# P*V of two key tiles back to back at each second key tile, in an attention and mixture-of-experts kernel on one core

## The reference, cut to what matters

```
kv = (ckv @ wkv_b)                       # ckv: 64 latent numbers per token
scores = einsum('bhqd,bhkd->bhqk', qs, ks_) * scale
scores = where(causal, scores, min)
attn = softmax(scores, axis=-1)
out = einsum('bhqk,bhkd->bhqd', attn, v)
return out @ wo
```

## Time and profile before

| what | value |
|---|---|
| time, median of 3 runs | 1330.67 us (1329.75 to 1333.64) |
| span of the profiled execution, first to last instruction | 1335.4 us |
| own time of the profiled execution | not recorded beside its span |
| PE busy | 1184.3 us, 89% |
| DVE, ACT, POOL busy | 61%, 60%, 55% |
| mean granted TensorE clock | 0.968 |

### The profile page before, as it was taken

One profiled execution on the slowest core, in us unless ns is written; L12 is line 12 of the kernel. 1 busy time (PEld: TensorE's weight loads), 2 busy tenths in 40 slices (PEclk: granted clock), 3 DMA queues, 4 the chain that ended last, 5 costly groups with the idle time before them and its releaser, 6 DMA issues. The chain is left out here.

```text
span 1335.4 us, 20034 instructions
## 1 busy us (share of the span) xinstructions
PE 1184.3 (89%) x6808; PEld 554.4 (42%) x6819; DVE 819.6 (61%) x1846; ACT 796.1 (60%) x1237; POOL 733.9 (55%) x444
## 2 busy tenths in 40 slices
PE   4988999999998999999999899999999999588820
PEld 3533555444443543434433533333333335266610
DVE  6565677657658765565657775566655516455546
ACT  3634663766664567666666467777777782265532
POOL 0055540564553266666676077878778891435545
PEclk9998999999999999999999999999999999799965
DMA  9035200110111010000011001000000000256744
GB/s 291 22 93 134 75 1 1 54 27 16 26 39 32 8 47 18 11 20 12 16 32 41 13 12 44 25 24 15 10 24 25 24 1 16 63 152 190 184 133 134
DMA packets 63031, 70.27 MB, mean 53 GB/s; under 512 B 10080, under 2 KB 52448, under 8 KB 62816
## 3 DMA queue, kind: packets, MB, share of 16 engines
q1 hardware_dynamic: 56656, 56.26, 14.8%
q0 software_dynamic: 4864, 10.51, 3.4%
q10 hardware_dynamic: 1424, 2.38, 0.7%
HBM read 37.51 MB, written 14.83 MB: 39 GB/s over the span
## 5 line engine op out<-in xcount | busy, mean ns | idle before, releaser
L561 POOL TENSOR_TENSOR D<-D,B 128x1024 f32<-128x1024 f32 (+3 forms) x256 | 513.0, 2004 | 140.8 <-ACT B L753 124.1
L1114 DVE TENSOR_REDUCE mxp<-ps 128x1 f32<-128x512 f32 (+3 forms) x640 | 385.4, 609 | 272.3 <-PE ps L1661 196.5
L753 ACT ACTIVATE B<-ps 128x1024 f32<-128x1024 f32 (+1 forms) x320 | 286.0, 894 | 224.2 <-PE ps L1690 150.6
L1711 PE MATMUL ps<-B,kv 128*64 128x512 f32 (+3 forms) x1280 | 303.2, 553 | 1.9 <-ACT C L640 0.9
L640 ACT ACTIVATE ps<-D 128x1024 f32<-128x1024 f32 (+3 forms) x327 | 288.3, 883 | 24.7 <-DVE D L1130 15.0
L1690 PE MATMUL ps<-A,KTh 128*128 128x512 f16 (+3 forms) x768 | 208.3, 353 | 2.9 <-ACT ps L640 2.9
L554 POOL TENSOR_TENSOR D<-B 128x1024 f32<-128x1024 f32 (+1 forms) x32 | 70.9, 2217 | 228.2 <-ACT B L753 228.2
L1661 PE MATMUL ps<-KTh,A 128*128 128x512 f16 (+3 forms) x384 | 135.7, 356 | 7.5 <-DVE mxp L1114 7.3
L1690 PE MATMUL ps<-A,KTl 128*128 128x512 f16 (+3 forms) x384 | 135.3, 352 | 0.0
L1690 PEld LDWEIGHTS ps<-A,KTh 128*128 128x128 f16 x768 | 63.7, 98 | 97.6 <-issue 51.2
L1711 PEld LDWEIGHTS ps<-B,kv 128*64 128x64 f32 x1280 | 63.7, 134 | 89.4 <-issue 73.8
(11 more groups left out here) (271 smaller groups left out, 1776.8 us busy)
## 6 DMA issues: line engine op xcount, KB each, us to landing
results<-B SPq DMA_DIRECT2D x64, 128.0 KB
xnTl<-in_L_ffn_experts_gate_up SPq DMA_DIRECT2D x16, 256.0 KB, 2.8
A<-in_L_attn_wq SPq DMA_DIRECT2D x4, 768.0 KB, 21.2
B<-in_L_attn_x SPq DMA_DIRECT2D x5, 512.0 KB, 5.8
D<-in_L_attn_wo SPq DMA_DIRECT2D x2, 1024.0 KB, 19.2
A<-C SPq DMA_DIRECT2D x16, 128.0 KB, 2.3
A<-C SPq DMA_DIRECT2D x32, 64.0 KB, 2.0
A<-stg SPq DMA_DIRECT2D x16, 128.0 KB, 2.3
```

Of the source, the lines that this page charges most:

```text
L561: nc.gpsimd.tensor_tensor(acc[:, :, c0:], acc[:, :, c0:], Pr[:, kt % P_RING, :, c0:], ALU.add).then_inc(sum_done, 1)
L753: nc.scalar.activation(Pr[:, kt % P_RING, :, c0:], ps[:, 2 * (kt % ST_RING):2 * (kt % ST_RING) + 2, c0:], ACT.Exp, scale=SM_SCALE).then_in ...
L1114: V.tensor_reduce(mxp[:, s, i4, kc:kc + 1], ps[:, BK_X + j % MX_RING, 0:w], AX.X, ALU.max).then_inc(mx_free, 1)
L1711: ins = T.matmul(ps[LORA * s:LORA * (s + 1), BK_O, c0:], kv[:, kt, 0:LORA], Pr[:, kt % P_RING, s, c0:], start=(kt == 0), stop=(kt == KT - 1))
```

## The change

The condition `kt >= LAG` is replaced by one on odd key tiles: nothing of `values` stands at even key tiles, and at an odd tile `kt` stand tiles `kt - 3` and `kt - 2`, one behind the other (at `kt = 1` they are the last two of the pair of heads before).

```
-                    if kt >= LAG:
-                        values(qc, p, kt - LAG)
-                    elif p:
-                        values(qc, p - 1, KT - LAG + kt)
+                    if kt % LAG:
+
+                        for v in range(kt - LAG - 1, kt - 1):
+                            if v >= 0:
+                                values(qc, p, v)
+                            elif p:
+                                values(qc, p - 1, KT + v)
                     between(3 * kt + 2)
```

## The result

The changed kernel takes **1325.82 us** (median of 6 runs, 1323.89 to 1328.07), the kernel before in the same comparison 1332.24 (6 runs, 1329.75 to 1337.37): ratio **0.9952**, 95% interval 0.9933 to 0.9970. It is 6.4 us faster, where 16.9 were forecast. The profiled execution of the changed kernel took 1328.07 us with a span of 1326.3, so 1.8 us lie around the span; by that the profiled execution of before (span 1335.4) was its slowest. Runs with a clearly lower granted clock (one of e5, 1553.59 us at 0.74, and one of the kernel before beside it, 1445.69 us at 0.83) are left out of all ratios.

The account below looks back on a forecast made before the run. TensorE's own pace was taken to bound the attention; 39.0 us from joins less 22.1 us of waits leaves 16.9 us, so 1330.7 falls to about 1314 us, range 1300 to 1326 (8 in 10).

Parts of the forecast that it names:

- the price of a join: Going in and out of `values` costs TensorE 0.25 us a group; 156 joins give 39.0 us.
- (a): Even tiles: the third slot's unit, with no `values` before it, waits about 0.09 us for a reduction; 5.5 us together.
- (b): 8 even pairs of blocks 1 and 2: slot 8 and the first spread wait; 0.62 a pair, 5.0 us.
- (c): 6 odd pairs of blocks 1 and 2: slot 8's projection waits for VectorE's rotation, also the first spread; 8 us.
- (d): Block 0: the second spread waits for the row of maxima (L1122), 0.37 us a pair, 2.6 us for seven.
- (e): Last pair of block 0, first of blocks 2 and 3, which wait already: 1 us by feel, from 0 to 4.
- ScalarE, the score ring and GpSimd: New TensorE waits for ScalarE's seeds, score buffers or GpSimd: taken as 0.
- the waits take it all: Rival: new waits in the attention lose 35 to 43 us, time around 1330 us; chance 0.10.
- the ring of two: Rival: the maxima's ring binds at even tiles' third slot, 0.78 us each, 1370 us, half way 1340; chance 0.06.

Follow-up runs that it names:

- e5: Changed kernel with the products of tiles 0 and 2 back at key tiles 2 and 4 in odd pairs of blocks 1 and 2: 1316.74 us, 0.9903.
- e7: Changed kernel with a 128-column matmul of zeros on the full array between the two tiles of each group in block 3: 1342.66 us, 1.0108.
- e2: Changed kernel with the second spread of block 0 in a bank of the maxima ring, not the first spread's: 1321.42 us, 0.9937.
- e3: Changed kernel, but in block 0 the product of tile 0 stands alone at key tile 2, as before: 1319.95 us, 0.9928.
- e8: Kernel before, with the second spread of block 0 in a bank of the maxima ring: 1330.88 us, ratio 1.0012.
- e6: Changed kernel, old order at some tiles of block 0 and odd pairs of blocks 1-2, and in first pairs of blocks 2-3: 1306.70 us, 0.9827.
- e4: Changed kernel with the old order in the last pair of block 1 and the first pairs of blocks 2 and 3: 1323.47 us, 0.9951.

## Why the prediction was wrong

The direction was right and so was the price of a join: 156 joins at 0.25 us, which the 1.87 us of a group and e7 confirm. What failed is the sum of the waits. It said 22.1 us; joins of 39.0 less the 6.6 gained in the trace leave 32.4. By the prediction's terms (joins at 0.25 us, changes from the table above; block 3 with the -1.69):

| term | forecast | measured |
|---|---|---|
| (a) third unit | 5.5 (3.5 of it in block 3) | 2.3 in block 3; in blocks 1 and 2 it is inside (b) and (c) |
| (b) even pairs of blocks 1 and 2 | 5.0 | 4.7 (seven pairs) |
| (c) odd pairs of blocks 1 and 2 | 8.0 | 12.6 |
| (d) block 0, pairs 0 to 6 | 2.6 | 7.5 |
| (e) last pair of block 0, first of blocks 2 and 3 | 1.0 | 5.3 |
| sum | 22.1 | 32.4 |

Three terms, (c), (d) and (e), are each too small by 4 to 5 us, and (a) hides 3 us of that. The measured 1325.82 lies within the stated 1300 to 1326 by 0.2 us, and that is luck: the gain was 6.4 where 16.9 were forecast.

**(d), block 0: the step that failed in kind.** The prediction let the second `spread` wait for the row of maxima, L1122, and put 0.37 us on it. The code also makes it wait for the widening of the first, whose bank it shares (`wide_done`, plus `s`). In the trace of before that wait is just covered: it shows once, with 0.2 us, and in the rows of the place itself not at all. In the changed kernel it is 1.07 us a pair, in seven pairs. e2 takes the bank away and is left with the wait of L1124 (0.56 rather than 0.37), e3 puts the cover back, e8 shows that the bank cost nothing before. That is 4.9 of the 10.3 us missing. Block 0 as a whole was to gain 0.5 us and lost 4.7.

**(c), odd pairs: mechanism right, count wrong.** With joins of 1.0 us in block 1 and a change of +0.25, a pair loses 1.27 us, and 1.3 was forecast; in block 2 it is 1.6. But the last pair of a block rotates queries as well, so there are eight of them and not six, which is 3.2 us. In block 1's odd pairs the second `spread` has lost its cover too: in pair 1 it starts 0.47 us late (0.30 in the row), which (c) didn't have and which e5 keeps, whose gain is in the first half of the pair.

```profile
280.12 0.38 PE L1672 MATMUL ps<-c,mrow 128*128 128x128 bf16 x4 [0.30 <-DVE mrow L1122]
```

And in pair (1,3) a transpose (L1595) stands behind the second `spread`'s widening, which itself stands behind L1170. TensorE, then VectorE in the changed kernel:

```profile
327.92 0.38 PE L1672 MATMUL ps<-c,mrow 128*128 128x128 bf16 x4 [0.30 <-DVE mrow L1122]
...
329.56 0.55 PE L1595 MATMUL ps<-c,WEh 128*128 128x128 f32 x3 [1.03 <-DVE D L1130]
```

```profile
327.69 1.23 DVE L1170 TRANSPOSE_TENSOR_REDUCE Lp<-D 128x32 f32<-128x1024 f32 x1
328.85 0.65 DVE L1130 COPY D<-ps 128x512 f32<-128x512 f32 x1
```

Before, TensorE waited there for 0.6 us, now for 1.03, and for L1122 besides. That its cover at key tile 6 was part of it is shown by e6, where tile 4 stands there again (24.40 against e5's 25.07).

**(e), a guess of 1 us.** Block 2's first pair has lost its 1.3 us of joins and 0.8 more, block 3's first its 1.8 and 0.6. In the last pair of block 0, joins of 0.5 and 0.5 more are lost to a wait for a reduction:

```profile
199.43 0.67 PE L1661 MATMUL ps<-KTh,A 128*128 128x512 f16 x2 [0.62 <-DVE mxp L1114]
```

e3 still has it, and its pair takes 41.01 us against 40.68 before and 41.16 changed. Together (e) is 5.3, above the 0 to 4 that was allowed for. e4 and e6 settle block 2's (32.90 in both). For block 3's first pair I have no profile with the old order and a full clock but that of before; there TensorE's waits for L1114 went from 5.3 us (3) to 6.3 (5) and those for seeds from 0.4 to 0.9, and the rest of its loss is argued by likeness.

**(b), even pairs: right.** 0.62 us of loss was forecast; block 2 shows joins of 1.5 less 0.88, 0.62 (its first pair is in (e)). The rows of pair 2 of block 1 show both waits, 0.23 us at slot 8 and 0.31 at the first `spread`. But there and in pair 4 some 0.9 is lost, since the work at the end of the pair now waits 0.34 for the widening as well (L1595 in pair 2):

```profile
303.62 0.65 PE L1595 MATMUL ps<-c,WEh 128*128 128x128 f32 x4 [0.18 <-DVE D L1130]
```

**(a), the third unit: right in kind, too dear.** In pair 1 of block 3 waits of 0.09 stand at three even tiles, and one of 0.14 where the second unit is a narrow one. Such a pair loses 0.24 (8 joins of 0.254, gain of 1.79), not 0.5. And for blocks 1 and 2 the 0.09 was counted in (b) a second time. Block 3 as a whole gained 11.1 us, and 11.5 was forecast.

**ScalarE, the score ring and GpSimd** were put at 0 and stayed near it: the waits for seeds went from 6.1 to 6.8 us. (In block 3 GpSimd with 270 us, and not ScalarE with 263, comes next behind TensorE. Nothing hangs on that slip of the prediction.) In this profile the clock did not fall: blocks 1 to 3 stand at 1.00 with the new waits too. The rival "the waits take it all" was nearest in outcome, but by places that it didn't name; the ring of two did not become the bound.

By blocks the forecast was too high by 5.2 us in block 0, 2.4 in block 1, 2.4 in block 2 and 0.4 in block 3.

## What to carry to other kernels

A group of matmuls on the half-width array cost its way in and out here, 0.25 us, and joining two such groups gave it back wherever TensorE waited for nobody. But in an order where two other engines' answers are just in time, every piece that is moved is also a cover that is taken away: for each place that loses its cover, list every wait that the program puts there, those with no row in the trace above all, and take the latest. Then join only where nothing is waited for: that made 23 us of 6.

## What was not expected of the hardware

The length of a pair of heads repeats to 0.01 us between profiles of different kernels (pair 1 of block 3 takes 41.35 or 41.36 in seven of them), while the rest of the program varies: from the last exponentials to the end it took 220.0 to 231.4 us in the ten profiles, although nothing behind the attention had been changed. So pairs, not spans, could tell these orders apart. In six of the ten profiles one or two stretches of 3.4 us at half the granted clock fell into the first pair of block 3, where TensorE waits up to 2.8 us for VectorE (e4: at 767.6 and 781.3), with the old order and the new alike, and in the other four none. With the old order that pair took 45.44 us without such a stretch (before), 45.90 and 47.08 with one (e6, e8), and 47.71 with two (e4).
